# Narrow attention rearranged: head pairs in 64-row tiles, operand rows stacked in DRAM, value products one slot later

## The reference

```
x = x + _L0_attn_b_ref(_layernorm(x, axis=-1), ...)      # unmasked
...
x = x + _L2_attn_b_ref(_layernorm(x, axis=-1), ...)      # causal

def _L0_attn_b_ref(x, Wq, bq, Wk, bk, Wv, bv, Wo, bo):
    ...
    q = proj(Wq, bq)
    k = proj(Wk, bk)
    v = proj(Wv, bv)
    score = jax.nn.softmax(jnp.einsum('bhif,bhjf->bhij', q, k) / SCALE, axis=-1)
    attn = jnp.einsum('bhij,bhjf->bihf', score, v)
    o = attn.reshape(b, n, f) @ Wo.T + bo
    return o
```

## Time and profile before

| | us |
|---|---|
| median of 3 runs | 3666.92 (3662.32 to 3667.54) |
| profiled execution, time | 3659.59 |
| profiled execution, span of its instructions | 3657.6 |
| PE / DVE / ACT / POOL busy in the span | 2741.8 / 1890.3 / 1451.8 / 558.9 |
| first L0b stage, first LayerNorm matmul of it to that of the next stage | 271.7 to 469.9 |
| first L2b stage, likewise | 1170 to 1343 |

### The profile page before, as it was taken

One profiled execution on the slowest core, in us unless ns is written; L12 is line 12 of the kernel. 1 busy time (PEld: TensorE's weight loads), 2 busy tenths in 40 slices (PEclk: granted clock), 3 DMA queues, 4 the chain that ended last, 5 costly groups with the idle time before them and its releaser, 6 DMA issues. The chain is left out here.

```text
span 3657.6 us, 33867 instructions
## 1 busy us (share of the span) xinstructions
PE 2741.8 (75%) x12082; PEld 1218.6 (33%) x12082; DVE 1890.3 (52%) x2639; ACT 1451.8 (40%) x2368; POOL 558.9 (15%) x324
## 2 busy tenths in 40 slices
PE   3565769899878579466746657789997877894677
PEld 1221145445344234123212211554443433341232
DVE  4867642455122751595649586415552237416955
ACT  2442511555234244343524424125552433443434
POOL 0533000000003101161006320000000040011600
PEclk8897977999989799799968979689999898997999
DMA  2001000000010210000000020000000102100000
GB/s 91 0 1 39 15 0 1 1 1 1 0 46 1 44 50 6 0 1 1 1 13 0 0 43 11 1 1 1 1 1 0 46 9 41 51 0 0 0 1 6
DMA packets 31504, 48.18 MB, mean 13 GB/s; under 512 B 7520, under 2 KB 19808, under 8 KB 31328
## 3 DMA queue, kind: packets, MB, share of 16 engines
q1 hardware_dynamic: 31328, 45.93, 4.8%
HBM read 38.18 MB, written 7.34 MB: 12 GB/s over the span
## 5 line engine op out<-in xcount | busy, mean ns | idle before, releaser
L1598 ACT ACTIVATE L1b_pr<-ps,L1b_mneg 128x512 f32<-128x512 f32 x256 | 173.8, 684 | 195.7 <-DVE L1b_mneg L1637 195.7
L518 POOL TENSOR_TENSOR xs<-xs,L2f_part 128x512 f32<-128x512 f32 x32 | 40.5, 1264 | 1287.6 <-DVE L2f_part L507 1287.6
L1356 ACT ACTIVATE L0b_pt<-ps 128x1024 f32<-128x1024 f32 x128 | 129.6, 1024 | 209.4 <-PE ps L1294 209.4
L1635 DVE TENSOR_REDUCE L1b_m<-ps 128x2 f32<-128x1024 f32 x128 | 156.7, 1224 | 105.0 <-PE ps L1502 101.0
L90 ACT ACT_TABLE_LOAD x34 | 43.6, 1283 | 419.6 <-PEq L671 181.4
L1403 DVE TENSOR_REDUCE L0b_mx<-ps 128x1 f32<-128x512 f32 x256 | 161.2, 684 | 47.7 <-PE ps L1278 45.0
L1046 POOL TENSOR_TENSOR L0a_db<-L0a_du,L0a_bs 128x1024 f32<-128x1024 f32 x64 | 150.3, 2353 | 227.8 <-ACT L0a_bs L1017 217.1
L1046 POOL TENSOR_TENSOR L3a_db<-L3a_du,L3a_bs 128x1024 f32<-128x1024 f32 x64 | 150.3, 2353 | 226.5 <-ACT L3a_bs L1017 216.0
L1356 ACT ACTIVATE L2b_pt<-ps 128x1024 f32<-128x1024 f32 (+3 forms) x128 | 88.4, 704 | 204.2 <-PE ps L1297 203.7
L1278 PE MATMUL ps<-L0b_ks,L0b_qs 128*128 128x512 bf16 x256 | 104.0, 446 | 87.0 <-DMA L0b_ks<-parts_dram 51.8
L1661 DVE COPY L1b_prt<-ps 128x512 f32<-128x512 f32 x128 | 88.5, 691 | 125.0 <-PE ps L1513 124.7
(11 more groups left out here) (564 smaller groups left out, 5853.1 us busy)
## 6 DMA issues: line engine op xcount, KB each, us to landing
L2f_w<-expert_dram SPq DMA_DIRECT2D x32, 256.0 KB, 3.0
L2g_w<-expert_dram SPq DMA_DIRECT2D x32, 256.0 KB, 3.0
weights<-w_dram SPq DMA_DIRECT2D x7, 820.5 KB, 9.3
parts_dram<-L0b_cut SPq DMA_DIRECT2D x4, 768.0 KB, 3.3
L0b_qs<-parts_dram SPq DMA_DIRECT2D x96, 32.0 KB
L0b_ks<-parts_dram SPq DMA_DIRECT2D x96, 32.0 KB
parts_dram<-L2b_cut SPq DMA_DIRECT2D x4, 768.0 KB, 3.3
L2b_qs<-parts_dram SPq DMA_DIRECT2D x96, 32.0 KB
```

The source lines that it names most:

```text
L1356: act.activation(pt[:, n % 3, 2 * half:2 * half + 2, q0:T], g.ps[:, 2 * (s % 2):2 * (s % 2) + 2, q0:T], ACT.Exp).then_inc(prob, 1)
L1598: act.activation(pr[:, s % 2, h, :], g.ps[:, 2 * (s % 2) + h, :], ACT.Exp, bias=mneg[:, s % 2, h:h + 1], accum_out=total[:, u % 2, t, h:h ...
L1635: dve.tensor_reduce(m[:, s % 2, :], g.ps[:, 2 * (s % 2):2 * (s % 2) + 2, :], AX.X, ALU.max).then_inc(max_raw, 1)
```

## The change

**Layout.** `qs` and `ks` hold two heads of a pair one above the other: head 0 in partitions 0 to 63, head 1 in 64 to 127, each with 48 stacked rows, two (no longer three) maximum rows and padding. The matmuls of tops and scores contract over 64 rows, and the two score matmuls of a slot use the two halves. Heads are dealt anew: the weights of q, k, v and the output are permuted on the host. The fills are written as float32 words over the bfloat16 tiles, 128x4096 instead of two times 128x8192 each.

**Parts.** Sequence 0 is cut by DVE, sequence 1 by POOL. The parts are duplicated while they are sent: six transfers for each of q and k put the stack in its final order into `stack_dram`, and a unit is fetched in four transfers of 48 partitions x 1024. For sequence 0 unit 0's rows go first, q on SP's queue and k on ACT's. The projections of the two sequences have banks of their own.

**Maxima.** DVE only negates; POOL cuts in two parts; SP writes four rows in four transfers.

**Products.** The product of a pair is issued one slot later (in odd slots), and where it is wider than 256 queries in two halves, with a top before each. `LEAD` is 28.

**End of eight products.** PE transposes the sums (4 matmuls of 128x128), DVE takes the reciprocal of 128x32 and multiplies, PE transposes back, ACT adds the bias while copying. The output of the first sequence is computed in slot 43.

```diff
-    AHEAD = 2
-    LEAD = 25
+    LEAD = 28
...
+        def send(q, b, x, j, i0, n, landed):
+            part = (Q_PART, K_PART)[x][j]
+            dst = g.stack_dram[b, x, i0:i0 + n, :, :, j, :, :].rearrange("i r f c t -> (i r f) (c t)")
+            q.dma_start(dst, cut[32 * i0:32 * (i0 + n), b, part, x, :]).then_inc(landed, 16)
+
+        def load(q, u, x, landed):
+            b, i = u // 4, u % 4
+            for r in range(2):
+                q.dma_start((qs, ks)[x][HALF * r:HALF * r + ROWS, b, 2 * i:2 * i + 2, :],
+                            g.stack_dram[b, x, i, r, :, :, :, :].rearrange("f j c t -> (f j) c t")).then_inc(landed, 16)
...
+                for j in Q_ORDER:
+                    sp.wait_ge(cut_dve, Q_PART[j] + 1)
+                    send(sp, 0, 0, j, 0, 1, first_q)
+                sp.wait_ge(filled, 2)
+                sp.wait_ge(first_q, SENDS)
+                load(sp, 0, 0, stacked)
...
+                    pe.wait_ge(ln.done, b + 1)
+                    qb, kb, vb = ((0, 1, 2), (3, 6, 7))[b]
...
                     for x in range(2):
-                        r, bank = 2 * half + x, 2 * (s % 2) + x
-                        mm = pe.matmul(g.ps[:, bank, q0:T], ks[:, b, i, r, kt * P:(kt + 1) * P], qs[:, b, i, r, q0:T],
-                                       start=True, stop=not causal)
+                        r, bank = HALF * x, 2 * (s % 2) + x
+                        mm = pe.matmul(g.ps[:, bank, q0:T], ks[r:r + HALF, b, 2 * i + half, kt * P:(kt + 1) * P],
+                                       qs[r:r + HALF, b, 2 * i + half, q0:T], start=True, stop=not causal)
...
-                    if s % 2 == 0 and s >= 2:
-                        products(s // 2 - 1)
...
+                    if s % 2 == 1 and s >= 3:
+                        n = (s - 3) // 2
+                        pieces = 2 if T - first(n % 4) > 2 * P else 1
+                        for x in range(pieces):
+                            if late:
+                                a = late.pop(0)
+                                top_scores(a // 17, a % 17)
+                            products(n, pieces, x)
...
+                for j in K_ORDER:
+                    act.wait_ge(cut_dve, K_PART[j] + 1)
+                    send(act, 0, 1, j, 0, 1, first_k)
+                act.wait_ge(filled, 2)
+                act.wait_ge(first_k, SENDS)
+                load(act, 0, 1, first_k_in)
+                for j in K_ORDER:
+                    send(act, 0, 1, j, 1, 3, more_k)
...
-                for b in range(NB):
-                    for j, dst in ((0, qs), (1, ks)):
-                        pool.memset(dst[:, b, :, :, :], float(j)).then_inc(ones_in, 1)
-                        pool.wait_ge(ones_in, 2 * b + j + 1)
+                pool.memset(qs_fill[:, :, :, :], 0.0).then_inc(filled, 1)
+                pool.memset(ks_fill[:, :, :, :], ONES_PAIR).then_inc(filled, 1)
+                pool.wait_ge(cut_dve, PARTS)
...
+                for u in range(UN):
+                    pool.wait_ge(top_in, 17 * u + 17)
+                    if u >= 2:
+                        pool.wait_ge(m_rows, 64 * (u - 1))
+                    pool.tensor_copy(mcut[:, u % 2, 0, :], mt[:, u % 2, :]).then_inc(m_hi, 1)
...
-                    dve.reciprocal(inv, g.ps[:, 6 + c % 2, :]).then_inc(inv_ready, 1)
+                    dve.reciprocal(inv[:, :, :], rows[:, :, :, DH]).then_inc(inverse, 1)
```

More of the change, by code:

```diff
@@ L1221, in _ @@
                 st.clear_spent(sp)
[L1223 to L1228, removed]
-                    b, i = u // 4, u % 4
[L1230 to L1233, removed]
-                    sp.wait_ge(stacked, STACK * (u + 1))
@@ new lines, in _ @@
+                for j in Q_ORDER:
[4 more added lines that the diff above has]
+                load(sp, 0, 0, stacked)
+                for j in Q_ORDER:
+                    send(sp, 0, 0, j, 1, 3, more_q)
+                sp.wait_ge(more_q, SENDS)
+                sp.wait_ge(more_k, SENDS)
+                sp.wait_ge(stacked, LOADS // 2)
+                for x in range(2):
+                    load(sp, 1, x, stacked)
@@ new lines, in products, with turn, turn_back @@
+                    if x == pieces - 1:
+                        mm.then_inc(pv, 1)
+                def turn(c):
+                    pe.wait_ge(copied, c + 1)
+                    for t in range(KT):
+                        mm = pe.transpose(g.ps[:, 6 + c % 2, t * P:(t + 1) * P], acc[:, c % 2, t * P:(t + 1) * P], g.w("ident"))
+                    mm.then_inc(turned, 1)
+                def turn_back(c):
+                    pe.wait_ge(scaled, c + 1)
+                    for t in range(KT):
+                        mm = pe.transpose(g.ps[:, 6 + c % 2, t * P:(t + 1) * P], att[:, t, :, :].rearrange("p n x -> p (n x)"), g.w("ident"))
+                    mm.then_inc(back, 1)
@@ L1320, in _, with output @@
+                def output(b):
+                    pe.wait_ge(at_ready, 2 * b + 2)
+                    for c in range(2):
+                        mm = pe.matmul(g.ps[:, 7, :], g.w(w + "_wo", c * P, P), at(2 * b + c), start=(c == 0), stop=(c == 1))
+                    mm.then_inc(out_ready, 1)
                 for a in range(LEAD):
                     top_scores(a // 17, a % 17)
-                for s in range(8 * UN):
+                pe.wait_ge(proj_in, 2 * NB)
+                pe.wait_ge(v_in, NB)
@@ L1338, in _ @@
+                products(4 * UN - 1, 1, 0)
+                turn(2 * NB - 1)
+                turn_back(2 * NB - 1)
+                output(NB - 1)
             @block.scalar
@@ L1434, in _, with output @@
+                def output(b):
+                    dve.wait_ge(out_ready, b + 1)
+                    dve.scalar_tensor_tensor(out=g.xs[:, b, :], in0=g.ps[:, 7, :], scalar=g.w(w + "_bo"), in1=g.xs[:, b, :],
+                                             op0=ALU.add, op1=ALU.add).then_inc(added, 1)
+                for a in range(LEAD):
                     maxima(a // 17, a % 17)
-                for s in range(8 * UN):
+                for s in range(SLOTS):
                     for a in range(tops_before(s), tops_before(s + 1)):
@@ L1437, in _ @@
                         maxima(a // 17, a % 17)
[L1438 to L1444 removed]
+                    if s % 16 == 6 and s > 16:
+                        divide(s // 16 - 1)
```

281 lines of the change are left out of this document (150 added, 131 removed).

## The result

The changed kernel takes **3630.5 us** (median of four runs, 3624.5 to 3631.7). The kernel before took 3665.4 us on the same chip (3662.3 to 3667.5). The ratio is 0.990, with an interval of 0.989 to 0.992. So it is faster by 35 us, or 1.0%. The forecast was 196 us, and the time lies 88 us above the upper end of its range. The profiled execution has a span of 3630.3 us.

The account below looks back on a forecast made before the run. PE and DVE were taken to hold each other up, neither full. Savings of 51.2 us in L0b and 46.9 in L2b, twice each, make 196: 3659.6 becomes 3463.4, plus 7.3 for the median gives 3471 us, range 3436 to 3542.

Parts of the forecast that it names:

- Start of a stage: L0b and L2b before the first top: faster conversions and earlier sends, 19.5 us less a stage (17.7 to 21.5).
- First tops: Tops before the first slot: 28 instead of 25 cost 0.7 us more in L0b, no change in L2b.
- Middle of L0b: L0b's slots with tops: 13.3 us per unit of 17 tops (12.3 to 15.5), 28.2 us less a stage.
- Last slots and output: Stage ends: L0b's last 13 slots 14.8 instead of 15.8 us; output 3.2 us less in L0b, 1.6 in L2b.
- Middle of L2b: L2b's slots: 10.9 us a unit (9.7 to 13.2), with 12.3 for the end slots 25.8 us less a stage.
- the prediction's own signs of being wrong: Forecast wrong if a unit stays above 15.5 us, PEclk is near 0.5 in the slots, or scores wait for maximum rows.
- TensorE stays at its lower clock: Rival: half-height matmuls count less for the clock, 1.2 GHz throughout the slots, kernel 3691 us, slower; chance 0.04.
- The second case of the forecast: Rival in L0b and L2b: 64-row halves don't overlap or tile-shape changes drain, 63 us more, 3534 us; chance 0.2.
- that rival: Maximum rows come late through slow POOL instructions and landings: 1 us a unit, 3503 us; within the first case's range.

## Why the prediction was wrong, point by point

- **Start of a stage: right.** First top at 291.6 us, forecast 292.4. The conversions took 0.69 us each instead of up to 6.11, the rows were sent from 281.8 us, and the transfers landed after 2.2 us, between the bounds. L2b gained the same: 38.8 us before its first top became 18.5.
- **First tops: right in L0b,** 19.1 us for 28, as forecast (18.4 and 0.7). In L2b they took 18.2 us instead of an unchanged 16.2.
- **Middle of L0b: 6 us short.** 108 tops in 90.7 us, forecast 84.5: 14.3 us a unit instead of 13.3. At 2.4 GHz it was 13.7 (some 80 tops in 64.7 us). The rest is that the first 14.4 us of slots ran at 1.2 GHz, which the forecast left out of the unit.
- **Last slots and output: right to a us.** L0b's slots took 14.8 us, as forecast, and its output 6.8 up to the next stage's first matmul (the row above ends 1.2 us later), forecast 7.9. L2b's took 12.7 and 9.0 us, forecast 12.3 and 7.9; the clock fell to 0.61 in its output.
- **Middle of L2b: the step that failed.** 10.9 us a unit were put down, 21.0 were measured (133.4 us for 108 tops): 64 us too little, of the 67.8 by which the stage was missed. Between the two profiled executions 169 us were missed (27 us less instead of 196): 135 in L2b, 9 in L0b and 25 in stages that the forecast left as they were. Two of the prediction's own signs of being wrong came true here, a unit above 15.5 us and PEclk near 0.5 in the slots.

Two things are wrong in that step. The sum took PE's work at 2.4 GHz. The rival *TensorE stays at its lower clock* had the place and nearly the price, 18.4 us a unit (its own terms, 9.7 and 8.2, make 17.9), and got a chance of 0.04, because PE's busy share would be higher than before. The trace refutes that reason: 132.0 of 133.0 us busy, clock 0.54. The slots at 1.2 GHz without changes of tile around the tops took 18.3 us a unit, the rival's price almost to the digit. Its mechanism, that 64-row work counts for less, is not the main one either. With all scores, tops and masks at 64 rows the clock is granted (133 us), and in L0b, where half-height tops and scores run too, it is 1.00.

The second error is what made the rival's case true. The masks were priced as columns, 32 x 0.054, "nothing gained". That they stay 128 rows high between scores of 64 rows was not counted as changes of tile; only eight changes around products were. A unit has 16 tops and 8 score pairs, each with a change to its masks and mostly one back. At 0.11 us, 32 changes around the tops alone would be 3.5 us; 2.7 were measured, which is what 21.0 has above the rival's 18.4. With one tile shape and the clock granted a unit took 11.0 us (12.0 where it holds the transposes of the sums), close to the 10.9 forecast: the rest of the step was sound. In the kernel before, all of these tiles were 128 rows high.

The second case of the forecast asked whether the halves overlap. They do: at 2.4 GHz in L0b a pair of 512 columns takes 0.39 us, as long as a single one.

```profile
351.05 0.39 PE L1313 MATMUL ps<-L0b_qs,L0b_ks 64*128 64x512 bf16 x2
352.44 0.39 PE L1297 MATMUL ps<-L0b_ks,L0b_qs 64*128 64x512 bf16 x1 [0.57 <-DVE L0b_mx L1489]
```

And each change of tile costs 0.11 us, less than the 0.15 assumed. The Trainium skill (TensorEngine Tiling (Array Packing), Key Properties) says that a change of mode drains TensorE. The gap of 0.11 us between score and mask agrees, at either clock, and the units above show that the clock costs more here than the gaps, 6.2 us against 3.8. The Trainium skill (TensorE: Matmul & The Clock Gate, A second HAM failure mode: psum-queue depth-cycling) tells of frequent short idle stretches that make the clock oscillate. The runs with paired tops agree, where PE waited between pairs and the clock went up and down. In the changed kernel's L2b the gaps are shorter, and the clock did not oscillate: it stayed at 1.2 GHz for 143 us.

Shown: changes of tile between scores and masks made the loss. Three edits that remove them, all or those around the tops, bring the clock and give 55 to 61 us a stage, about six tenths of it by the clock and four by the changes themselves. They hold the clock back by degrees: in L2b it rose after 158 us with all of them, after 82 and 120 without those around the tops, and after 38 to 52 with none between scores and masks; in L0b, masks put in moved the rise from 52 to 117 us but didn't keep it away. Not shown: whether the clock answers to the gaps themselves or to something that goes with a change. Maximum rows were waited for nowhere to speak of, and POOL's short instructions took 0.28 to 0.42 us, so that rival never came in.

## What to carry to other kernels

When a change makes some matmuls half as high, look at every matmul that stands between them. If a mask or a transpose keeps the full height, each neighbour is a change of tile: 0.11 us here, and with nearly fifty of them in each unit of 21 us the higher clock was not granted, although PE was busy all the time by its records. Give them one shape, even at the price of more matmuls, before you judge the half-height form. And do not argue from PE's busy share that the clock will be high: price each stage at both levels, and give the lower one a real chance wherever its matmuls become shorter, lower or more mixed.

## What was not expected of the hardware

- PE was busy 99% by its records through 121 us of slots (1170 to 1291 us) and was granted 1.2 GHz. The same slots without tops got 2.4 GHz.
- Adding full-height work can delay the clock: 128-row masks in L0b moved the rise from 52 to 117 us after the stage's start.
- The clock also moves in stages that no edit touched. L1b took 290.6 or 290.7 us in both passes before and 297.2 in both after. Twenty microseconds of it in the changed kernel, pass 1:

```profile
613.00:633.00 20.00, 17.96 (x73) 9.42 (x74) 9.06 (x14) 9.73 (x25) 0.00 (x0) 0.77 0.00 0
```

And with products in one piece in L2b:

```profile
613.00:633.00 20.00, 18.48 (x106) 9.78 (x106) 10.87 (x18) 13.59 (x35) 0.00 (x0) 1.00 0.00 1
```

L1b took one of these two lengths in each pass of every profiled execution here. Why is open. It can move a total by 7 or 13 us, so differences of that size between two kernels say nothing of the edit until the stages are compared.
